# The order of all steps on four engines, and the table of shared PSUM banks, set anew in a hand-scheduled adaLN block

## The reference

```python
x = L0_attn_embeddings
mod = (_silu(L0_c) @ L0_wmod).reshape(L0_c.shape[0], 6, 1, -1)
sa, ca, ga, sb, cb, gb = (mod[:, 0], mod[:, 1], mod[:, 2], mod[:, 3], mod[:, 4], mod[:, 5])
ga = (2 * (ga >= 0) - 1) * jnp.maximum(jnp.abs(ga), 0.25)
gb = (2 * (gb >= 0) - 1) * jnp.maximum(jnp.abs(gb), 0.25)
h = _layernorm(x, axis=-1) * (1 + ca) + sa
x = x + ga * _L0_attn_ref(h, L0_attn_guidance_trajectories)
h = _layernorm(x, axis=-1) * (1 + cb) + sb
x = x + gb * _L0_ffn_ref(h, L0_ffn_wqkv, L0_ffn_q_scale, ...)
return x
```

## Time and profile before

| | |
|---|---|
| median of 3 runs | 829.01 us (828.92 to 829.85) |
| the profiled execution | 828.6 us |
| its span | 826.8 us |
| mean granted clock of TensorE | 0.99 |
| busy: TensorE, ScalarE, VectorE, GpSimd | 739.7, 651.9, 642.8, 560.0 us |
| HBM read and written | 6.67 MB, 2.10 MB |

### The profile page before, as it was taken

How to read it: one execution, slowest core, us unless ns; L and a number is a source line. 1 busy time by engine, 2 the same in 40 slices (tenths; PEclk the granted TensorE clock), 3 DMA queues, 4 the chain that set the end, 5 groups by cost and what they waited for, 6 DMA issues and landing times.

```text
span 826.8 us, 20278 instructions
## 1 busy us (share of the span) xinstructions
PE 739.7 (89%) x7391; PEld 544.2 (66%) x7391; DVE 642.8 (78%) x1575; ACT 651.9 (79%) x1543; POOL 560.0 (68%) x428
## 2 busy tenths in 40 slices
PE   5698799988999998898989999999989999998885
PEld 4576566665776766666667776666667767666753
DVE  4859886877897977778889887687889966867742
ACT  3166858889998976989897887888898988788863
POOL 2277791978987861786997872487899871877801
PEclk9999999999999999999999999999999999999996
DMA  7000000000000000000000100000000000000000
GB/s 246 2 14 15 1 2 1 1 2 2 1 2 27 2 1 27 2 2 2 2 1 2 27 1 27 2 2 2 1 2 2 15 1 15 1 2 2 2 14 13
DMA packets 12713, 10.05 MB, mean 12 GB/s; under 512 B 1088, under 2 KB 11720, under 8 KB 12616
## 3 DMA queue, kind: packets, MB, share of 16 engines
q1 hardware_dynamic: 12616, 8.77, 3.5%
...
HBM read 6.67 MB, written 2.10 MB: 11 GB/s over the span
## 4 chain that ended last, share of the span: by engine, by line
PE 37%; ACT 19%; POOL 19%; issue 12%; DVE 12%; DMA 1%; POOLq 0%; SPq 0%; ACTq 0%; DVEq 0%
ACT probs L1148 7%; PE pair L842 6%; POOL qk L1713 6%; POOL roots L1658 5%; PE dense L997 4%; PE mixed L888 4%; POOL qk L1704 3%; ACT probs_t L1156 3%; PE pair L928 2%; PE dense L988 2%; PE dense L985 2%; PE dense L1079 2%; PE dense L986 2%; PE dense L1082 2%; PE mixed L953 1%
## 5 line engine op out<-in xcount | busy, mean ns | idle before, releaser
L1658 POOL TENSOR_TENSOR roots<-powers,minus_half 128x16 f32<-128x16 f32 (+1 forms) x65 | 191.9, 2952 | 5.3
L1713 POOL TENSOR_TENSOR qk<-qk,turned_s 128x512 f32<-128x512 f32 x128 | 168.1, 1330 | 7.4 <-DVE turned_s L1592 5.4
L1148 ACT ACTIVATE probs<-pair,neg_max 128x128 f32<-128x128 f32 x512 | 139.2, 410 | 9.2 <-DVE neg_max L1409 8.5
L1592 DVE TENSOR_TENSOR turned_s<-dense,tables 128x512 f32<-128x512 f32 x128 | 87.5, 683 | 24.5 <-ACT qk L1273 22.9
L1079 PE MATMUL dense<-wq_hi,h_hi 128*128 128x512 f32 x192 | 90.3, 470 | 15.0 <-DVE turned_s L1592 7.6
L1704 POOL TENSOR_TENSOR qk<-qk,tables 128x512 f32<-128x512 f32 x64 | 83.1, 1302 | 29.4 <-ACT qk L1273 29.3
L1409 DVE TENSOR_REDUCE neg_max<-pair 128x4 f32<-128x512 f32 x128 | 81.1, 683 | 22.6 <-PE pair L928 22.3
L1269 ACT ACTIVATE squares<-dense 128x512 f32<-128x512 f32 x128 | 78.5, 615 | 19.0 <-PE dense L1082 13.7
L842 PE MATMUL pair<-eye_s,probs 128*128 128x128 f32 x512 | 76.0, 279 | 14.3 <-ACT probs L1148 13.9
L1597 DVE TENSOR_REDUCE powers<-squares 128x8 f32<-128x512 f32 x128 | 86.5, 676 | 0.0
L1391 DVE TENSOR_TENSOR qk<-qk,roots 128x1024 f32<-128x1024 f32 x64 | 82.3, 1287 | 1.0 <-POOL roots L1658 1.0
...
## 6 DMA issues: line engine op xcount, KB each, us to landing
...
```

What stands on the lines that cost most here:

```text
L1148: last = act.activation(probs[:, ring, hh, :], banks[m][:, hh * P:(hh + 1) * P], ACT.Exp, bias=neg_max[:, ring, hh:hh + 1], scale=1.0)
L1592: dve.tensor_tensor(turned_s[:, t % 2, m, :].rearrange("p (h a b) -> p h a b", h=HEADS, a=2), halves[:, :, ::-1, :], rot(layer, t, 2 * m + 1),
L1658: return pool.tensor_tensor(to, of, minus_half[0:of.shape[0], 0:of.shape[-1]], ALU.pow)
L1713: pool.tensor_tensor(part, part, turned_s[:, t % 2, m, :], ALU.add).then_inc(added, 1)
```

## The change

It rewrites `ORDER` for all four engines and `BANK_OF_USE`, and nothing else. Each engine's list has the same steps as before, each once. In another position are 432 of 957 steps on TensorE, 354 of 787 on ScalarE, 295 of 683 on VectorE and 115 of 339 on GpSimd; most by a few places. The farthest: VectorE's 0/3:proj.keep 44 places later, 3/2:proj.keep 38 and 3/3:proj.keep 35 earlier, 2/3:proj.unit.3 16 earlier; ScalarE's 1/0:proj.tile.3.2 15 later; TensorE's 4/1:proj.tile.1.2 14 and 1/0:proj.tile.0.2 12 later. Of the 400 bank digits 262 differ. Parts of the diff, first TensorE, then ScalarE, VectorE and GpSimd (of GpSimd's middle the lines around 3/2:proj.split and 3/2:ff.hi):

```diff
         -1/3:setup.silu -1/3:setup.mod -1/3:new.turn -1/3:setup.guide -1/3:new.dots -1/3:setup.warm.0
         -1/3:setup.gate -1/3:new.mix -1/3:new.sum -1/3:setup.rows -1/3:setup.warm.1 -1/3:setup.warm.2
-        -1/3:new.stream -1/3:setup.warm.3 0/2:new.turn 0/2:proj.tile.0.0 0/2:proj.tile.0.1 0/2:proj.tile.0.2
+        -1/3:new.stream 0/2:new.turn -1/3:setup.warm.3 0/2:proj.tile.0.0 0/2:proj.tile.0.1 0/2:proj.tile.0.2
         0/2:proj.tile.1.0 0/2:proj.tile.1.1 0/2:proj.tile.1.2 0/2:new.dots 0/2:proj.tile.2.0 -1/3:setup.warm.4
-        -1/3:setup.warm.5 -1/3:setup.warm.6 0/2:proj.tile.2.1 0/2:new.mix 0/2:proj.tile.3.0 0/3:a.turn.0.0
-        0/2:new.sum 0/2:proj.tile.3.2 0/3:a.turn.0.1 0/3:a.turn.1.1 0/3:a.turn.1.0 0/2:proj.tile.2.2
-        0/2:proj.tile.3.1 0/3:a.score.0 0/3:a.score.1 0/3:a.flip.0.0 0/2:new.stream 0/3:a.flip.0.1 -1/3:setup.warm.7
...
+        -1/3:setup.warm.5 0/2:proj.tile.2.1 -1/3:setup.warm.6 0/3:a.turn.0.1 0/2:new.mix 0/2:proj.tile.3.0
+        0/2:new.sum 0/3:a.turn.0.0 0/3:a.turn.1.0 0/3:a.turn.1.1 0/2:proj.tile.3.2 0/2:proj.tile.2.2 0/3:a.score.0
+        0/2:proj.tile.3.1 0/3:a.score.1 0/3:a.flip.0.0 0/2:new.stream 0/3:a.flip.0.1 -1/3:setup.warm.7 0/3:a.mix.0.0
...
+        0/3:proj.tile.0.2 0/3:a.turn.2.0 0/3:new.turn 0/3:proj.tile.2.0 0/3:proj.tile.2.1 0/3:proj.tile.1.2
+        0/3:a.out.1 0/3:new.dots 0/3:a.turn.3.0 0/3:a.turn.3.1 0/3:proj.tile.3.0 0/3:a.score.2 0/3:a.score.3
...
         -1/3:setup.silu -1/3:new.turn -1/3:new.dots -1/3:setup.hi.0 -1/3:setup.hi.1 -1/3:new.sims -1/3:new.mix
         -1/3:new.stream 0/2:proj.split 0/2:new.turn 0/2:proj.tile.0.0 0/2:proj.tile.0.1 0/2:proj.tile.0.2
-        0/2:proj.tile.1.0 0/2:proj.tile.1.1 0/2:proj.tile.1.2 0/2:new.dots 0/2:new.sims 0/2:proj.tile.2.0
-        0/2:proj.tile.2.1 0/2:new.mix 0/3:a.turn.0.0 0/2:proj.tile.3.0 0/3:a.turn.0.1 0/3:a.turn.1.1 0/3:a.turn.1.0
-        0/2:proj.tile.3.2 0/3:a.score.0.0 0/3:a.score.0.1 0/2:proj.tile.3.1 0/2:new.stream 0/3:proj.split
...
+        0/2:proj.tile.1.0 0/2:proj.tile.1.1 0/2:proj.tile.1.2 0/2:new.dots 0/2:proj.tile.2.0 0/2:new.sims
+        0/2:proj.tile.2.1 0/3:a.turn.0.1 0/2:new.mix 0/2:proj.tile.3.0 0/3:a.turn.0.0 0/3:a.turn.1.0 0/3:a.turn.1.1
+        0/2:proj.tile.3.2 0/2:proj.tile.2.2 0/3:a.score.0.0 0/3:a.score.0.1 0/2:proj.tile.3.1 0/2:new.stream
...
+        0/3:proj.tile.1.2 0/3:a.out.1 0/3:a.turn.2.0 0/3:new.dots 0/3:a.turn.3.0 0/3:a.turn.3.1 0/3:proj.tile.3.0
...
-        -1/3:setup.silu -1/3:new.stats -1/3:setup.square -1/3:new.turn -1/3:setup.guide -1/3:setup.mod
-        -1/3:setup.wide -1/3:setup.dots -1/3:new.dots -1/3:new.sims -1/3:new.weights -1/3:setup.lo.0 -1/3:setup.lo.1
-        -1/3:setup.ff -1/3:setup.gate -1/3:new.gate -1/3:setup.columns -1/3:new.again 0/2:new.stats -1/3:new.stream
-        0/2:proj.keep 0/2:new.turn 0/2:proj.split 0/2:proj.tile.0.0 0/2:proj.tile.0.1 0/2:proj.tile.1.0
-        0/2:proj.tile.1.1 0/2:new.dots 0/2:new.sims 0/2:new.weights 0/2:proj.unit.0 0/2:proj.tile.2.0
-        0/2:proj.tile.2.1 0/2:proj.tile.3.0 0/2:proj.unit.1 0/2:new.gate 0/2:new.again 0/3:a.score.0.0
-        0/3:a.score.0.1 0/2:new.stream 0/3:proj.keep 0/3:new.stats 0/3:a.score.1.0 0/3:a.score.1.1 0/3:proj.split
...
+        -1/3:setup.silu -1/3:new.stats -1/3:new.turn -1/3:setup.square -1/3:setup.mod -1/3:setup.guide
+        -1/3:setup.dots -1/3:setup.wide -1/3:new.dots -1/3:new.sims -1/3:setup.gate -1/3:new.weights -1/3:setup.lo.0
+        -1/3:setup.lo.1 -1/3:setup.ff -1/3:new.gate -1/3:setup.columns -1/3:new.again 0/2:new.stats -1/3:new.stream
+        0/2:new.turn 0/2:proj.keep 0/2:proj.split 0/2:proj.tile.0.0 0/2:proj.tile.0.1 0/2:proj.tile.1.0
+        0/2:proj.tile.1.1 0/2:new.dots 0/2:new.sims 0/2:proj.tile.2.0 0/2:new.weights 0/2:proj.unit.0
+        0/2:proj.tile.2.1 0/2:proj.unit.1 0/2:proj.tile.3.0 0/2:new.gate 0/2:new.again 0/3:a.score.0.0
+        0/3:a.score.0.1 0/2:new.stream 0/3:a.score.1.0 0/3:a.score.1.1 0/3:new.stats 0/3:proj.split
...
+        1/0:a.mix.0.0 0/3:proj.keep 1/0:ff.hi 1/0:a.mix.0.1 1/0:a.mix.1.0 1/0:a.mix.1.1 0/3:proj.unit.2
...
-        -1/3:new.again 0/2:new.stats 0/2:proj.split 0/2:new.steps 0/2:proj.cos.0.0 0/2:proj.cos.1.0
-        0/2:proj.tile.0.0 0/2:proj.tile.0.1 0/2:proj.tile.1.0 0/2:new.dots 0/2:proj.rsqrt.0 0/2:proj.rsqrt.1
-        0/2:proj.cos.2.0 0/2:proj.tile.1.1 0/2:proj.tile.2.0 0/2:proj.tile.2.1 0/2:proj.rsqrt.2 0/2:proj.cos.3.0
-        0/2:new.again 0/2:proj.tile.3.0 0/3:new.stats 0/3:proj.split 0/2:proj.rsqrt.3 0/3:proj.cos.0.0
...
+        -1/3:new.again 0/2:new.stats 0/2:proj.split 0/2:new.steps 0/2:proj.cos.0.0 0/2:proj.tile.0.0
+        0/2:proj.tile.0.1 0/2:proj.cos.1.0 0/2:proj.tile.1.0 0/2:new.dots 0/2:proj.rsqrt.0 0/2:proj.rsqrt.1
+        0/2:proj.cos.2.0 0/2:proj.tile.1.1 0/2:proj.tile.2.0 0/2:proj.tile.2.1 0/2:proj.cos.3.0 0/2:new.again
+        0/2:proj.rsqrt.2 0/2:proj.tile.3.0 0/3:new.stats 0/3:proj.split 0/2:proj.rsqrt.3 0/2:proj.tile.3.1
...
-        3/1:proj.tile.3.0 3/1:proj.tile.3.1 3/1:proj.rsqrt.2 3/2:new.dots 3/2:proj.split 3/1:proj.rsqrt.3
...
-        3/2:proj.rsqrt.1 3/2:ff.hi 3/2:proj.tile.3.0 3/2:proj.tile.3.1 3/2:new.again 3/2:proj.rsqrt.2
...
+        3/1:proj.rsqrt.2 3/1:proj.cos.3.0 3/1:proj.tile.2.1 3/1:proj.tile.3.0 3/1:proj.tile.3.1 3/2:new.dots
+        3/1:proj.rsqrt.3 3/2:proj.split 3/2:proj.cos.0.0 3/2:proj.tile.0.0 3/2:proj.tile.0.1 3/2:proj.cos.1.0
...
+        3/2:proj.tile.2.1 3/2:proj.rsqrt.1 3/2:proj.rsqrt.2 3/2:ff.hi 3/2:proj.cos.3.0 3/2:new.again
+        3/2:proj.tile.3.0 3/2:proj.rsqrt.3 3/2:proj.tile.3.1 3/3:proj.split 3/3:proj.cos.0.0 3/3:proj.tile.0.0
...
 BANK_OF_USE = (
-    "0120120120121020120102102112012012120122012012021212012012012102101201201202102101201012102210210212"
...
+    "0120120120121020112012012010221021021200121210202102102102102012021202102021021012021021210021021021"
```

More of the change, by code:

```diff
@@ new lines @@
+        2/3:new.mix 2/3:proj.tile.3.2 3/0:a.turn.0.0 2/3:ff.norm 2/3:a.out.3 2/3:ff.up.1 2/3:ff.up.0 2/3:ff.up.2
+        3/0:a.turn.1.0 3/0:a.turn.1.1 3/0:ff.stats 2/3:store.scale 3/0:a.score.0.0 3/0:a.score.0.1 3/0:a.score.1.0
+        3/0:a.score.1.1 3/0:a.flip.0.0 3/0:a.flip.0.1 3/0:a.flip.1.0 3/0:a.flip.1.1 2/3:new.stream 3/0:ff.norm
+        3/0:ff.up.0 3/0:a.turn.2.1 3/0:ff.up.1 3/0:a.out.0 3/0:a.out.1 3/0:ff.up.2 3/0:a.turn.2.0 3/0:a.turn.3.0
+        3/0:a.turn.3.1 3/0:proj.split 3/0:a.score.2.0 3/0:a.score.2.1 3/0:proj.tile.0.0 3/0:proj.tile.0.1
@@ L346 @@
-        1/3:a.mix.3.0 1/3:a.mix.3.1 1/3:new.dots 1/3:new.sims 1/3:ff.norm 1/3:new.weights 1/3:ff.hi 1/3:proj.unit.1
-        1/3:a.project 1/3:proj.tile.3.1 1/3:new.gate 1/3:ff.up.0 1/3:ff.up.1 2/0:a.score.0.0 2/0:a.score.0.1
-        1/3:ff.up.2 1/3:new.again 1/3:ff.down 2/0:a.score.1.0 2/0:a.score.1.1 1/3:store.turn 2/0:ff.stats
-        1/3:new.stream 2/0:ff.norm 2/0:a.mix.0.0 2/0:a.mix.0.1 1/3:proj.keep 2/0:ff.hi 2/0:a.mix.1.0 2/0:a.mix.1.1
-        1/3:proj.unit.2 2/0:ff.up.0 2/0:ff.up.1 2/0:ff.up.2 1/3:proj.unit.3 2/0:ff.down 2/0:proj.split
@@ new lines @@
+        0/3:proj.tile.0.1 0/3:proj.tile.1.0 0/3:proj.tile.1.1 0/3:a.mix.1.0 0/2:proj.unit.3 0/3:a.mix.1.1
+        0/3:proj.tile.2.0 0/3:proj.tile.2.1 0/3:new.dots 0/3:new.sims 0/3:a.score.2.0 0/3:a.score.2.1
+        0/3:proj.tile.3.0 0/3:new.weights 0/3:a.score.3.0 0/3:a.score.3.1 0/3:a.mix.2.0 0/3:a.mix.2.1 0/3:a.mix.3.0
+        0/3:a.mix.3.1 0/3:proj.unit.0 0/3:proj.unit.1 0/3:new.gate 0/3:new.again 0/3:proj.tile.3.1 0/3:a.project
+        1/0:a.score.0.0 1/0:a.score.0.1 1/0:a.score.1.0 1/0:a.score.1.1 1/0:ff.stats 0/3:new.stream 1/0:ff.norm
@@ new lines @@
+        1/3:proj.tile.2.1 1/3:a.score.2.0 1/3:a.score.2.1 1/3:a.score.3.0 1/3:a.score.3.1 1/3:proj.tile.3.0
+        1/3:ff.stats 1/3:proj.unit.0 1/3:a.mix.2.0 1/3:a.mix.2.1 1/3:a.mix.3.0 1/3:a.mix.3.1 1/3:new.dots
+        1/3:new.sims 1/3:ff.norm 1/3:new.weights 1/3:ff.hi 1/3:proj.unit.1 1/3:a.project 2/0:a.score.0.0
+        2/0:a.score.0.1 1/3:proj.tile.3.1 1/3:new.gate 1/3:ff.up.1 1/3:ff.up.0 1/3:proj.unit.2 1/3:ff.up.2
+        1/3:new.again 1/3:ff.down 2/0:a.score.1.0 2/0:a.score.1.1 1/3:store.turn 2/0:ff.stats 1/3:new.stream
@@ new lines @@
+        2/2:ff.norm 2/2:proj.tile.3.1 2/2:ff.hi 2/2:a.mix.3.0 2/2:a.mix.3.1 2/2:new.gate 2/2:new.again 2/2:ff.up.0
+        2/2:new.stream 2/2:ff.up.2 2/2:ff.up.1 2/2:proj.unit.2 2/3:proj.split 2/2:ff.down 2/3:a.score.0.0
+        2/3:a.score.0.1 2/3:a.score.1.0 2/3:a.score.1.1 2/2:proj.unit.3 2/3:proj.tile.0.0 2/3:proj.tile.0.1
+        2/2:a.project 2/3:proj.tile.1.0 2/3:proj.tile.1.1 2/2:store.turn 2/2:proj.keep 2/3:a.mix.0.0 2/3:a.mix.0.1
+        2/3:a.mix.1.0 2/3:a.mix.1.1 2/3:new.stats 2/3:ff.stats 2/3:new.turn 2/3:proj.tile.2.0 2/3:ff.norm
```

700 lines of the change are left out of this document (340 added, 360 removed).

## The result

The changed kernel takes 823.36 us (median of 4 runs, 821.94 to 823.55), the kernel before 829.43 in the same comparison. The ratio is 0.9921, 95% interval 0.9907 to 0.9935, that is 0.8% faster: 6.1 us between the medians, 6.5 by the ratio. The profiled execution took 823.55 us, its span is 821.8.

The account below looks back on a forecast made before the run. TensorE was nearest its limit, with 87.1 us idle for an order to change; in the middle no engine bounds alone. The lead through 0/3 gave −4.5, middle and end 0: 824.1 profiled, 824.5 as median; range 819.5 to 829.5.

Parts of the forecast that it names:

- Start to new.dots: Lead-in: VectorE does setup.dots ahead of setup.wide, so new.dots starts at about 12.57 instead of 13.91, −1.34 us.
- Gate rows: Lead-in: VectorE's gate copies move into idle time before new.weights; setup.rows follows new.sum near 31.4, −2.5 us.
- the clock as a rival: TensorE's clock falls ahead of new.stream or the first projections: +1.6 us, 826.1; chance 0.10.
- warm.3: 0/2:new.turn ahead of these 20 filler turns: first projection loses 0.45 us, costed at nothing because of the h_lo wait.
- Projections of 0/2: Behind the first projection: GpSimd's root for new.dots comes 1.15 us earlier, giving −3.6 us at the filler turns of 77.34.
- 0/3: 80 to 100 us: turned q rows earlier on ScalarE; walked as −5.3 or −3.6 us in all, taken as −4.5.
- Middle: 127 to 800 us: more cover steps against late GpSimd steps, ends −4 and +4.7 us, taken as 0.
- GpSimd's late steps: Middle: in five places a long GpSimd step goes ahead of one others wait for; lateness sums to 4.7 us.
- the slower rival: Late GpSimd steps pass on in full, +4.7 us, and only 2.0 of the lead-in is kept: 831.7; chance 0.16.
- End: From the last attention on: same chain, 12.7 us of idle time stay, 0 us.
- Banks: Whole kernel: 262 of 400 digits naming the bank of a use change, costed at nothing.

Follow-up runs that it names:

- experiment 1: Kernel before with the new order only for the lead-in up to new.stream and 0/2:new.turn, old order and banks behind: 831.55 us, ratio 1.0028 to the kernel before.
- experiment 9: Kernel before with new order and banks for all steps the changed kernel starts before 125 us: 824.71 us, ratio 0.9945 to the kernel before.
- experiment 11: Changed kernel with the old order and banks for what it starts from 470 us on: 822.54 us, ratio 0.9909 to the kernel before.
- experiment 4: Changed kernel plus 30 filler turns between setup.gate and new.mix and 12 behind warm.2, ahead of new.stream: 820.03 us, ratio 0.9886 to the kernel before.
- experiment 6: Changed kernel with the old order and banks for what the kernel before starts before 43 us: 822.72 us, ratio 0.9918 to the kernel before.
- experiment 10: Kernel before with new order and banks for all behind the steps it starts before 128 us: 827.91 us, ratio 0.9980 to the kernel before.
- experiment 7: Kernel before with one GpSimd step moved, 0/2:proj.cos.1.0 behind 0/2:proj.tile.0.1: 827.81 us, ratio 0.9979 to the kernel before.
- experiment 8: Kernel before with the new order only for 0/3 steps, from 80 to 125 us: 828.50 us, ratio 0.9989 to the kernel before.
- experiment 12: Changed kernel with 30 and 12 filler turns in both lead-in gaps and the old order from 470 us on: 818.65 us, ratio 0.9860 to the kernel before.

## Why the prediction was right, and where it was not

The time lies 1.1 us under the forecast of 824.5, inside the range. The direction was right, and so was the view that an order can only take from TensorE's idle time in single places. That the number came so near is luck. In the profiled executions I had a lead of 4.5 us and it is 5.0, and between them lie errors of both signs: −2.8 at the first projection, +1.6 in the projections of 0/2, +2.3 in 0/3, −1.6 by the second fall of the clock, +1.4 in the middle, −0.4 in the last turn.

**Start to new.dots: right.** Forecast 12.57, measured 12.44.

**Gate rows: refuted.** The sum had −2.5 us at the first projection; it came 0.3 later. VectorE did what the forecast says. The step that failed is "it now runs right behind new.sum, at about 31.4": setup.rows came at 34.04, since the sums ahead of it ran at half clock. The pause that stands before this fall was in my own walk. I had TensorE's gates done at 21.95 and new.weights starting "about 0.1 earlier", so new.mix would have stayed near 26.1, 4.1 us behind the gates, where the kernel before has 2.93 (23.29 to 26.21). I didn't subtract them. Measured are 21.17 and 25.29, both some 0.8 earlier than that because warm.0 took 2.43 us instead of 3.11, and the pause is 4.12. The clock then stayed at 0.50 for 12 us in which the sums are on the path. I had the clock as a rival, at +1.6 and 0.10, but for a pause of 0.5 us ahead of new.stream; it came elsewhere, in all four profiles that have the pause of 4.12 us (the changed kernel, experiments 1, 9 and 11), and took 2.4 us of the 2.5 (the first projection at 44.55 in the changed kernel and 42.13 in experiment 4, though new.mix began 0.9 earlier in the changed kernel, at 25.29 against 26.18). It is not that pause alone: with the old lead-in the pause is shorter and the clock fell there in some profiles too (experiments 6 and 10: 0.69 and 0.59 from 26 to 30), where the old order waits for VectorE anyway. By the Trainium skill's rule that I cited ("the default state is throttled, and activity releases the throttle", page "TensorE: Matmul & The Clock Gate", section "What's actually happening") the pause was the thing to look at. The trace agrees: 0.50 from 26 us on behind the 4.12 us, and 1.00 in experiment 4, where 0.85 us of it are left. With the pauses filled, new.stream came at 38.29 and the projection at 42.13, where I had about 38.2 and 42.2: the walk was right about all but the clock, and about warm.0, which it took as fixed.

**warm.3: right.** The third product of the first tile waits 0.61 us for h_lo still (45.90), and 0.33 in experiment 4, where the lead-in is at full clock. So the filler's place costs nothing.

**Projections of 0/2: right mechanism, too small.** I had −1.1 us behind the first projection; the rows give −2.7 (from +0.3 there to −2.4 at warm.7). Here my term was too small by 1.6. GpSimd's move is worth the 1.15 (experiment 7); the other 1.5 us came with the moves on ScalarE, TensorE and VectorE, to which I gave nothing of their own. Which of them was not tried.

**0/3: too small.** I took a further −0.9, with −1.7 as the end; the rows give −3.2 at score.2 (a lead of 2.4, then 5.6). Alone it gave 1.8 (experiment 8). The second fall of the clock then took 1.6 back, which no term had.

**Middle: wrong as a net of two.** I took 0, between −4 and +4.7. It gained 3.8 us up to 476 (a lead of 4.0, then 7.8) and lost 2.4 behind: 1.4 us gained in all. The counts of steps were the better evidence for the first part; my argument that two windows of before were equally idle was not, since those of the new order differ, 11.0 and 12.4.

**GpSimd's late steps: there, but not the 4.7 us.** The split of h at 3/2 starts right behind a root, and ff.hi too (kernel after):

```profile
591.32 2.93 POOL L1659 TENSOR_TENSOR roots<-powers,minus_half 128x16 f32<-128x16 f32 x1
594.22 1.27 POOL L1698 TENSOR_TENSOR h_lo<-shifted,h_hi 128x512 fp32r<-128x512 f32 x1
...
620.07 2.93 POOL L1659 TENSOR_TENSOR roots<-powers,minus_half 128x16 f32<-128x16 f32 x1
622.97 1.28 POOL L1682 TENSOR_TENSOR hn_lo<-hn,hn_hi 128x512 fp32r<-128x512 f32 x1
```

Against the earlier trace rows they are 5.1 and 4.8 us earlier, where TensorE around them was 6.4 and 6.2 earlier: 1.4 us late each, as I had 1.1 and 1.4. TensorE had other steps to do: over the whole kernel its matmuls idle 3.3 us for h_lo and 1.7 for hn_lo, 3.1 and 1.4 before. This is the group of the third product:

```profile
L1083 PE MATMUL dense<-wq_hi,h_lo 128*128 128x512 f32 x192 | 76.9, 401 | 3.4 <-POOL h_lo L1698 3.3
```

So the slower rival, 4.7 us from these steps, is out. A smaller cost is not. Behind 470 us the new order costs 1.7 us against the old one (experiment 12), and the stretch of the late steps is where most of it goes: between 570 and 690 us the lead of the changed kernel falls from 7.2 to 5.5, that of experiment 11, with the old order there, only from 6.0 to 5.9. The old order gives up its part of the lead, 1.3, right behind the join. TensorE's own idle time for h_lo and hn_lo from 570 to 700 is the same in both, 0.6 and 0.2 us, so if GpSimd's steps cost this, they do it through other waits. No run moves them alone, and which steps do it stays open.

**End: right.** The chain of the last 20 us is the same; the last turn waits 1.78 us for ScalarE in both. It runs at half clock in the kernel after (four products of 128x128 in 1.07 us, 0.66 before), which takes 0.4 of the lead.

**Banks.** The digits were never changed alone, so that they cost nothing is not shown.
